# A decoder layer on one core: the softmax's divisors from a matrix product, Ln and Exp instead of VectorE's sums and reciprocal

## The chip, the cores and the metric

The kernel runs on one core of one Trainium2 chip. The metric is device time in microseconds (us) of one execution. Engines: TensorE (PE; its weight loads are shown apart as PEld), VectorE (DVE), ScalarE (ACT), GpSimd (POOL) and SyncE (SP), which only issues transfers.

## What is computed

A decoder layer over 4 sequences of 1024 rows with 256 features: a gated recurrence with one state per head (16 heads of 16), cross attention to 77 rows of context, and a feed-forward part with 2 shared and 8 routed experts, of which each row uses two. A layer norm follows each. The change touches the cross attention:

```python
q = (x @ Wq.T).reshape(B, Sq, H, Dh).transpose(0, 2, 1, 3)
k = (y @ Wk.T).reshape(B, -1, H, Dh).transpose(0, 2, 1, 3)
v = (y @ Wv.T).reshape(B, -1, H, Dh).transpose(0, 2, 1, 3)
scores = jnp.einsum('bhqd,bhkd->bhqk', q, k)
scores = jnp.where(attention_mask == 0, -1e9, scores)
attn = jax.nn.softmax(scores / sqrt(Dh), axis=-1)
out = jnp.einsum('bhqk,bhkd->bhqd', attn, v)
return out.transpose(0, 2, 1, 3).reshape(B, Sq, Dall) @ Wo.T + bo
```

The output of the recurrence enters the residual only for rows from the 683rd on; the rest of the layer does not wait for it in the earlier rows.

## The kernel before

**Tiles and periods.** The 1024 positions are taken in 8 tiles of 128; a tile holds its 128 positions of all 4 sequences ("batches" b = 0 to 3). Tiles 0 to 4 are free: they need nothing of the recurrence. Tiles 5, 6 and 7 are bound: they add the recurrence's rows after a gate, a norm and a projection (`gate_rows`, `project_rows`). The recurrence runs on VectorE over 16 superblocks of 32 step pairs; two superblocks are a period, of 128 steps (t = 0 to 127), and between superblocks VectorE lays out the next one's vectors (`lay_out`, L1558, L1565). Period p does tile p for p = 0 to 4; period 5 has no tile of its own; periods 6 and 7 do tiles 5 and 6; tile 7 comes after the recurrence, alone. Superblocks from the 10th on also form outputs (L1584), which GpSimd sums (L1194 to L1202).

**Order on VectorE.** After every step VectorE calls `attention_after(t, ...)`, which does the piece of attention, norm or routing that is due at step t by the tables `FREE_AT` (free tiles) and `BOUND_AT` (bound tiles). The queue is in order: a piece that waits for another engine holds up the recurrence. Two successive steps are one pair; the pieces of both are done after the pair.

**Order on TensorE and ScalarE.** `last_experts` runs the last five experts of the tile before, with a part ahead of each: start (preparation of a superblock), attend (queries and scores), weigh (softmax and values), finish (projection `wo`), second (another preparation, which in free tiles waits for VectorE's residual). Then come the router, the two shared experts and the first three routed experts of the own tile (in bound tiles all eight). Each pass of a routed expert is a product (L642), a Gelu (L928), a product (L651) and a copy of the result (L934). ScalarE waits in `sums` (L943) for the store of the tile before, which follows its last norm. SP loads each expert's weights when the expert two places before it is done (L296, L297); in its queue stand also the stores of the recurrence's outputs (L325).

**The softmax.** ScalarE copies the scores to `probs` (L836). The smallest of each row (scores are negated) is found by VectorE (L1359). In tiles 0 to 4 and 7 (`SHIFTED`) GpSimd subtracts it (L1107), ScalarE takes one Exp per batch (L843), and VectorE sums the weights (L1366). In tiles 5 and 6 ScalarE does 16 Exp per batch with the accumulator as the sum (L847). TensorE transposes the weights by head (L506), ScalarE copies them to `eT` (L855), and TensorE multiplies them with the values (L514) in pairs of heads, 32 rows of a bank for two heads. VectorE takes the reciprocal of the sums (L1374) and copies it 16 times per head (L1376), TensorE transposes that (L525), ScalarE copies it out of its bank (L862), and VectorE multiplies (`divided`, L1383). TensorE projects (L533, L535), and VectorE adds the residual (L1333).

## Time and profile before

| | before |
|---|---|
| median of 3 runs | 2398.67 us (2394.86 to 2398.77) |
| profiled execution, its own time | 2398.25 us |
| its span | 2396.5 us |
| mean granted clock of TensorE | 0.842 of full speed |
| busy: TensorE, VectorE, ScalarE, GpSimd | 1760.5, 2050.7, 663.5, 1192.2 us |
| chain that ended last: VectorE, TensorE, GpSimd | 61%, 17%, 8% of the span |

The span runs from the first to the last recorded instruction; the execution's own time is 1.75 us longer. Times of rows are counted from the span's start.

### The profile page before, as it was taken

To read this page: it belongs to the slowest core of one execution; us is meant where nothing else is said; L and a number is where in the kernel's file an instruction comes from. 1 tells how busy PE (TensorE), PEld (TensorE's weight loads), DVE (VectorE), ACT (ScalarE), POOL (GpSimd) and SP (SyncE) were. 2 spreads that over 40 slices of the span, in tenths; PEclk is the share of its full clock that TensorE was granted. 3 is DMA by queue.
4 is the path that set the end of the run, shared out by engine and by line. 5 is a ranking of instruction groups with operands and counts; after the bars stand their busy time and mean duration, and the time that the engine had idled before them with its cause. 6 is when DMAs were issued, how large, how long until landed. Compare 5 with 4: busy or idle time off the path is not lost.

```text
span 2396.5 us, 31981 instructions
## 1 busy us (share of the span) xinstructions
PE 1760.5 (73%) x9438; PEld 1323.5 (55%) x9438; DVE 2050.7 (86%) x5770; ACT 663.5 (28%) x1457; POOL 1192.2 (50%) x1487
## 2 busy tenths in 40 slices
PE   4248988988698879886989440258797668877983
PEld 2135766676567666765667320145585436755673
DVE  5999999999999999999999998999996989924000
ACT  2122233323332333133312110161222711224121
POOL 2544354555455545554574469473763773304203
PEclk8568998999889979999899765567899669987997
DMA  7100342334324423343234220000245003540353
GB/s 260 37 1 13 133 142 82 117 134 141 104 83 141 141 80 112 137 139 107 79 110 164 82 93 14 20 1 5 97 155 190 18 1 108 171 161 18 104 171 112
DMA packets 175111, 238.53 MB, mean 100 GB/s; under 512 B 28657, under 2 KB 148074, under 8 KB 174954
## 3 DMA queue, kind: packets, MB, share of 16 engines
q1 hardware_dynamic: 140874, 194.46, 24.3%
q10 hardware_dynamic: 27936, 25.44, 3.3%
q0 software_dynamic: 6144, 16.79, 2.2%
q8 instruction: 68, 1.11, 0.2%
q14 instruction: 89, 0.73, 0.1%
HBM read 202.09 MB, written 33.16 MB: 98 GB/s over the span
## 4 chain that ended last, share of the span: by engine, by line
DVE 61%; PE 17%; issue 8%; POOL 8%; DMA 3%; ACT 2%; SPq 0%; POOLq 0%; ACTq 0%; DVEq 0%; PEldq 0%
DVE ps L1631 13%; DVE ps L1612 12%; DVE prod L1604 9%; DVE terms L1619 8%; DVE terms L1614 5%; PE ps L651 4%; PE ps L642 3%; PE ps L587 2%; PE ps L578 2%; DVE rec_out L1558 2%; DMA pj<-in_wpT 2%; DVE rec_in L1558 2%; DVE oprod L1584 2%; DVE stats L1318 1%; PE ps L434 1%
## 5 line engine op out<-in xcount | busy, mean ns | idle before, releaser
L1631 DVE TENSOR_REDUCE ps<-terms 128x64 f32<-128x320 f32 x1024 | 448.8, 484 | 0.0
L1612 DVE TENSOR_REDUCE ps<-prod 128x16 f32<-128x272 f32 x1024 | 397.4, 433 | 0.0
L1619 DVE TENSOR_TENSOR terms<-ps,rec_out 128x256 f32<-128x256 f32 x1024 | 381.8, 415 | 0.0
L1604 DVE TENSOR_TENSOR prod<-ps,rec_in 128x256 f32<-128x256 f32 x1024 | 380.9, 414 | 0.0
L642 PE MATMUL ps<-xg,fc 128*128 128x128 f32 x2848 | 353.9, 285 | 34.0 <-PE ps L651 12.0
L642 PEld LDWEIGHTS ps<-xg,fc 128*128 128x128 f32 x2848 | 343.5, 200 | 56.1 <-issue 48.5
L651 PE MATMUL ps<-pj,hT 128*128 128x256 f32 x1424 | 344.7, 397 | 33.3 <-ACT hT L928 33.3
L651 PEld LDWEIGHTS ps<-pj,hT 128*128 128x128 f32 x1424 | 273.3, 197 | 89.3 <-ACT hT L928 52.6
L578 PE MATMUL ps<-xtf,fc 128*128 128x512 f32 x512 | 246.0, 620 | 4.7 <-ACT vec L808 3.4
L587 PE MATMUL ps<-pj,hT 128*128 128x256 f32 x1024 | 237.4, 383 | 0.0
L587 PEld LDWEIGHTS ps<-pj,hT 128*128 128x128 f32 x1024 | 195.4, 191 | 57.3 <-issue 34.4
L1614 DVE TENSOR_TENSOR terms<-ps,rec_g 128x128 f32<-128x128 f32 x512 | 194.1, 379 | 0.0
L1035 POOL TENSOR_TENSOR rstd<-mv,ln_eps 128x4 f32<-128x4 f32 x19 | 3.9, 203 | 354.6 <-DVE mv L1322 354.6
L928 ACT ACTIVATE hT<-ps 128x512 f32<-128x512 f32 x178 | 104.1, 593 | 234.1 <-PE ps L642 234.0
L506 PE MATMUL ps<-ident,probs 128*77 128x128 f32 x512 | 92.5, 348 | 97.6 <-ACT probs L843 62.9
L1318 DVE BATCH_NORM_STATS2 stats<-y_out 128x6 f32<-128x256 f32 x32 | 11.2, 412 | 178.6 <-POOL y_out L1072 178.6
L1194 POOL TENSOR_TENSOR oprod<-oprod 128x128 f32<-128x128 f32 (+1 forms) x86 | 42.1, 490 | 237.8 <-DVE oprod L1584 237.7
L578 PEld LDWEIGHTS ps<-xtf,fc 128*128 128x128 f32 x512 | 101.0, 199 | 101.6 <-issue 90.4
L879 ACT ACTIVATE hT<-ps 128x512 f32<-128x512 f32 x128 | 76.4, 597 | 291.5 <-PE ps L578 291.3
L1055 POOL DMA_INDIRECT y_back<-out_rows,rows x64 | 63.1, 987 | 173.8 <-ACTq L948 158.8
L506 PEld LDWEIGHTS ps<-ident,probs 128*77 128x77 f32 x512 | 79.1, 195 | 112.0 <-issue 88.5
L934 ACT ACTIVATE y<-ps 128x256 f32<-128x256 f32 x89 | 34.2, 384 | 330.9 <-PE ps L651 330.9
(235 smaller groups left out, 3025.9 us busy)
## 6 DMA issues: line engine op xcount, KB each, us to landing
fc<-in_wfcT SPq DMA_DIRECT2D x80, 1024.0 KB, 5.2
pj<-in_wpT SPq DMA_DIRECT2D x80, 1024.0 KB, 8.2
xg_rows<-in_rows ACTq DMA_DIRECT2D x105, 128.0 KB, 2.1
out_rows<-y ACTq DMA_DIRECT2D x89, 128.0 KB, 5.7
in_rows<-o_rows SPq DMA_DIRECT2D x2, 2176.0 KB, 17.3
out_rows<-o_rows SPq DMA_DIRECT2D x2, 2176.0 KB, 16.9
xtp<-in_xT SPq DMA_DIRECT2D x32, 128.0 KB, 2.5
xin<-in_x SPq DMA_DIRECT2D x8, 512.0 KB, 6.7
```

The lines of the kernel that those rows point to most:

```text
L506: i = nc.tensor.transpose(ps[0:SK, TURNED[nth % len(TURNED)], h * P:(h + 1) * P], probs[:, b, q * QH + h], ident[:, :])
L578: ins = mm(ps[:, UP + g % 2, :], fc[:, par, c, g * P:(g + 1) * P], x2T[:, c], start=c == 0, stop=c == KC - 1)
L587: ins = mm(ps[:, ACC + b // 2, (b % 2) * D:(b % 2 + 1) * D], hT[:, g % 4, b * P:(b + 1) * P], pj[:, par, g], start=False, stop=e == NSH - ...
L642: i = mm(ps[:, UP + g // 4, g % 4 * P:(g % 4 + 1) * P], fc[:, par, c, g * P:(g + 1) * P], xg[:, c], start=c == 0, stop=c == KC - 1)
L651: i = mm(ps[:, UP + 1, 0:D], hR[:, g], pj[:, par, g], start=g == 0, stop=g == FG - 1)
L928: fn(hT[:, k], ps[:, UP + k, :], ACT.Gelu).then_inc(gelu_done, 1)
L1558: nc.vector.transpose(dst.rearrange("p n d -> p d n"), wide).then_inc(block_laid, 1)
L1604: tt(prod[:, c % PLACED, :, cols, 0:HD], SE[:, old, cols, 0:HD].unsqueeze(1).to_broadcast([P, NV, HC, HD]), rec_in[:, c].unsqueeze(2).to_b ...
L1612: red(SE[:, old, cols, HD:EH].rearrange("p v n -> p n v"), prod[:, c % PLACED, :, cols, 0:HD + 1], AX.X, ALU.add).then_inc(step_done, 1)
L1614: tt(terms[:, :, :, NV], SE[:, old, :, 0:HD], rec_g[:, c].unsqueeze(1).to_broadcast([P, HV, HD]), ALU.mult).then_inc(decayed, 1)
L1619: tt(terms[:, cols, :, 0:NV], SE[:, old, cols, HD:EH].unsqueeze(2).to_broadcast([P, HC, HD, NV]), rec_out[:, c].unsqueeze(1).to_broadcast( ...
L1631: red(SE[:, new, cols, 0:HD], terms[:, cols, :, 0:NV + 1], AX.X, ALU.add).then_inc(step_done, 1)
```

## The change

The sums of the weights come from TensorE: beside each product of the weights with a pair of heads' values there is one with `pair_ones`, of the same shape and with ones where the values were, so that each head's sum appears on that head's 16 rows of another bank. ScalarE takes Ln of the two banks and then Exp with scale -1, which gives the divisors where `divided` reads them. VectorE's sums, the reciprocal, the widening copy, TensorE's transposes of it and ScalarE's copy go. In tiles 5 and 6 Exp no longer writes the accumulator. In free tiles the divide moves from step 55 to 59 and the last norm from 110 to 112; in bound tiles everything from the divide on moves 4 steps earlier (the gathers 3).

```diff
@@ tensors @@
+        pair_ones = sb("pair_ones", [SK, 3 * HD])
-        weight_sum = sb("weight_sum", [P, B, H])
-        rden = sb("rden", [P, B, H])
-        rden_wide = qT.rearrange("p c (b h d) -> p (c b) h d", h=H, d=HD)
@@ TensorE @@
             def weigh_values(m, b):
                 pe.wait_ge(eT_sb, m * (4 * B) + (4 * b + 4))
+                if b == 0:
+                    pe.wait_ge(acc_sb, m * 2 + 1)
                 for h in range(H):
                     rows = slice(h % 8 // 2 * 2 * HD, (h % 8 // 2 + 1) * 2 * HD)
-                    i = mm(ps[rows, WEIGHED[h // 8], b * P:(b + 1) * P], vals[:, b, h // 2, h % 2 * HD:(h % 2 + 2) * HD], eT[0:SK, h], start=h % 2 == 0, stop=h % 2 == 1,
-                           tile_position=(0, rows.start))
-                    if b == B - 1 and h % 8 == 7:
-                        i.then_inc(attT_ps, 1)
-
-            def spread_sums(m):
-
-                pe.wait_ge(widened, m + 1)
-                pe.wait_ge(acc_sb, m * 2 + 1)
-                for c in range(KC):
-                    for b in range(B):
-                        i = nc.tensor.transpose(ps[:, ACC + c, b * P:(b + 1) * P],
-                                                rden_wide[:, b, c * 8:(c + 1) * 8].rearrange("p h d -> p (h d)"), ident[:, :])
-                    i.then_inc(spread_ps, 1)
+                    for bank, pair, done in ((WEIGHED[h // 8], vals[:, b, h // 2], attT_ps), (ACC + h // 8, pair_ones, spread_ps)):
+                        i = mm(ps[rows, bank, b * P:(b + 1) * P], pair[:, h % 2 * HD:(h % 2 + 2) * HD], eT[0:SK, h], start=h % 2 == 0, stop=h % 2 == 1,
+                               tile_position=(0, rows.start))
+                        if b == B - 1 and h % 8 == 7:
+                            i.then_inc(done, 1)
@@ ScalarE @@
-                    i = fn(probs[:, b, h], probs[:, b, h], ACT.Exp, bias=least[:, b, h:h + 1], scale=-1.0,
-                           accum_out=weight_sum[:, b, h:h + 1])
+                    i = fn(probs[:, b, h], probs[:, b, h], ACT.Exp, bias=least[:, b, h:h + 1], scale=-1.0)
-            def spread_sums(m):
+            def inverse_sums(m):
                 for c in range(KC):
                     act.wait_ge(spread_ps, m * 2 + (c + 1))
-                    fn(xtf[:, c], ps[:, ACC + c, :], ACT.Copy).then_inc(spread_sb, 1)
+                    fn(xtf[:, c], ps[:, ACC + c, :], ACT.Ln).then_inc(logged, 1)
+                for c in range(KC):
+                    act.wait_ge(logged, m * 2 + (c + 1))
+                    fn(xtf[:, c], xtf[:, c], ACT.Exp, scale=-1.0).then_inc(spread_sb, 1)
@@ VectorE @@
-            def sums_of_weights(t, m, at):
-            def divisors(t, m, at):
-                sums_of_weights(t, m, at["sums"])
-                divisors(t, m, at["divisors"])
+            for i in range(3):
+                nc.vector.memset(pair_ones[:, i * HD:(i + 1) * HD], float(i != 1)).then_inc(dve_const, 1)
@@ order @@
-FREE_AT = {1: 1, "caps": 46, "minima": (40, 42, 43, 44), "sums": (48, 48, 49, 50), "divisors": 51, "divided": 55, "resid": 65, 2: 65, "routing": 83, "gather": 82, "scatter": 92, "combine": 101, 3: 110}
-BOUND_AT = {"gated": 3, 0: 3, "x_plus": 12, 1: 13, "minima": (22, 22, 23, 24), "sums": (40, 40, 41, 41), "divisors": 42, "divided": 46, "resid": 53, 2: 53, "routing": 63, "gather": 30, "scatter": 74, "combine": 41, 3: 57}
+FREE_AT = {1: 1, "caps": 46, "minima": (40, 42, 43, 44), "divided": 59, "resid": 65, 2: 65, "routing": 83, "gather": 82, "scatter": 92, "combine": 101, 3: 112}
+BOUND_AT = {"gated": 3, 0: 3, "x_plus": 12, 1: 13, "minima": (22, 22, 23, 24), "divided": 42, "resid": 49, 2: 49, "routing": 59, "gather": 27, "scatter": 70, "combine": 37, 3: 53}
```

## Rows read from the trace of the kernel before

**Rows 1.** Busy time by stage: us, engines (instructions), clock, DMA share, GB/s.

```profile
600.00:840.00 240.00, 203.81 (x1152) 155.06 (x1150) 238.64 (x682) 76.99 (x149) 127.86 (x124) 0.93 0.35 117
```

**Rows 2.** Timeline, period 1 (tile 1): start, us, engine, line, [idle before].

```profile
384.36 1.12 PE L514 MATMUL ps<-eT,vals 77*32 77x128 f32 x32 [0.79 <-ACT eT L855]
385.42 0.69 DVE L1376 COPY qT<-rden 128x1024 f32<-128x1024 f32 x1
386.17 1.09 PE L525 MATMUL ps<-ident,qT 128*128 128x128 f32 x8 [0.69 <-DVE qT L1376]
389.37 0.57 ACT L928 ACTIVATE hT<-ps 128x512 f32<-128x512 f32 x1
392.19 1.28 DVE L1383 TENSOR_TENSOR xtf<-ps,xtf 128x512 f32<-128x512 f32 x2
...
412.05 2.08 PE L535 MATMUL ps<-c_o,xtf 128*128 128x256 f32 x4
417.65 1.27 DVE L1333 TENSOR_TENSOR x<-ps,x 128x512 f32<-128x512 f32 x2
448.59 0.19 DVE L1403 TENSOR_REDUCE rone<-rt 128x4 f32<-128x32 f32 x1 [0.38 <-ACT rt L868]
```

**Rows 3.** Timeline, tiles 2 to 4; last row: list of waits (us, times, longest).

```profile
660.28 1.01 PE L428 MATMUL ps<-xtp,w_f 128*16 128x128 f32 x4 [6.99 <-DVE x L1333]
847.85 1.23 ACT L843 ACTIVATE probs<-probs 128x1232 f32<-128x1232 f32 x1 [3.13 <-POOL probs L1107]
900.24 0.61 PE L428 MATMUL ps<-xtp,w_f 128*16 128x128 f32 x4 [2.15 <-DVE x L1333]
1139.86 1.01 PE L428 MATMUL ps<-xtp,w_f 128*16 128x128 f32 x4 [7.25 <-DVE x L1333]
...
PE ps L525 <- DVE qT L1376: 8.5, 5, 3.4
```

**Rows 4.** Timeline, end of period 4: VectorE and GpSimd.

```profile
1223.58 1.41 DVE L1318 BATCH_NORM_STATS2 stats<-y_out 128x6 f32<-128x256 f32 x4 [3.68 <-POOL y_out L1072]
1245.88 1.27 POOL L1172 TENSOR_TENSOR qbuf<-qbuf,fbuf 128x512 f32<-128x512 f32 x1
1249.61 1.19 DVE L1565 STREAM_TRANSPOSE vrec<-vec 128x256 f32<-128x256 f32 x2
```

**Rows 5.** Timeline, period 7 (tile 6): VectorE and ScalarE.

```profile
1843.56 1.29 DVE L1333 TENSOR_TENSOR xin<-ps,xin 128x512 f32<-128x512 f32 x2 [18.41 <-PE ps L470]
1917.68 1.09 ACT L862 ACTIVATE xtf<-ps 128x512 f32<-128x512 f32 x2 [1.80 <-PE ps L525]
1921.07 1.27 DVE L1383 TENSOR_TENSOR xtf<-ps,xtf 128x512 f32<-128x512 f32 x2
1936.36 1.28 DVE L1333 TENSOR_TENSOR x<-ps,x 128x512 f32<-128x512 f32 x2
1947.03 2.19 DVE L1326 TENSOR_SCALAR x<-x,mv,rstd 128x256 f32<-128x256 f32 x4 [3.91 <-POOL rstd L1037]
```

**Rows 6.** Timeline after the recurrence (tile 7).

```profile
2109.94 5.36 PE L642 MATMUL ps<-xg,fc 128*128 128x128 f32 x32 [3.40 <-DMA pj<-in_wpT]
2176.90 1.12 PE L514 MATMUL ps<-eT,vals 77*32 77x128 f32 x32 [0.79 <-ACT eT L855]
2179.35 1.29 DVE L1383 TENSOR_TENSOR xtf<-ps,xtf 128x512 f32<-128x512 f32 x2 [6.23 <-ACT xtf L862]
```

**Rows 7.** VectorE's groups by line and form: busy us, mean ns.

```profile
L1366 DVE TENSOR_REDUCE weight_sum<-probs 128x16 f32<-128x1232 f32 x24 | 33.3, 1429 | 1.6 <-ACT probs L843 1.6
L1376 DVE COPY qT<-rden 128x1024 f32<-128x1024 f32 x8 | 5.8, 723 | 0.3
L1374 DVE RECIPROCAL rden<-weight_sum 128x64 f32<-128x64 f32 x8 | 4.4, 550 | 0.6
```

**Rows 8.** ScalarE's groups by line and form.

```profile
L847 ACT ACTIVATION_READ_ACCUMULATOR probs<-probs,least 128x1 f32 x128 | 24.0, 188 | 0.0
L879 ACT ACT_TABLE_LOAD x17 | 21.8, 1283 | 0.3
```

More of the change, by code:

```diff
@@ L212, in decoder_layer @@
          kv_sb, sum_seen, prep_pool, block_laid, v_placed, step_done, decayed, o_terms, o_tree, o_sums, o_ready,
-         cap_done, x1T_ps, x1T_sb, q_ps, q_sb, sc_ps, sc_sb, capped, min_done, shifted, exp_done, summed, eT_ps,
-         eT_sb, rden_done, widened, attT_ps, spread_ps, spread_sb, attT_sb, wo_ps, resid, x2T_ps, doubled, x2T_sb, rt_ps, rt_sb,
+         cap_done, x1T_ps, x1T_sb, q_ps, q_sb, sc_ps, sc_sb, capped, min_done, shifted, exp_done, eT_ps,
+         eT_sb, attT_ps, spread_ps, logged, spread_sb, attT_sb, wo_ps, resid, x2T_ps, doubled, x2T_sb, rt_ps, rt_sb,
          route, w_done, picked, pos_ps, bounds_done, bounds_seen_pe, bounds_seen_act, gx_ps, gx_sb, xo1_ps,
@@ L220, in decoder_layer @@
             pool_set pool_const dve_const ctx_k_ps ctx_v_ps ctx_done prep_a_ps prep_b_ps xf1_sb fq_sb kv_sb
-            sum_seen prep_pool block_laid v_placed step_done decayed o_terms o_tree o_sums o_ready cap_done x1T_ps x1T_sb q_ps q_sb sc_ps sc_sb capped min_done shifted exp_done summed eT_ps eT_sb rden_done widened
-            attT_ps spread_ps spread_sb attT_sb wo_ps resid x2T_ps doubled x2T_sb rt_ps rt_sb route w_done picked
+            sum_seen prep_pool block_laid v_placed step_done decayed o_terms o_tree o_sums o_ready cap_done x1T_ps x1T_sb q_ps q_sb sc_ps sc_sb capped min_done shifted exp_done eT_ps eT_sb
+            attT_ps spread_ps logged spread_sb attT_sb wo_ps resid x2T_ps doubled x2T_sb rt_ps rt_sb route w_done picked
             pos_ps bounds_done bounds_seen_pe bounds_seen_act gx_ps gx_sb xo1_ps xo1_sb gate_ps gate_sb
@@ L713, in weigh @@
                             weigh_values(m, b)
-                        spread_sums(m)
                 def finish():
@@ L983, in weigh @@
                             turn_weights(m, b)
-                        spread_sums(m)
+                        inverse_sums(m)
                 def second():
@@ L1359, in minima @@
                         red(least[:, b], probs[:, b], AX.X, ALU.min).then_inc(min_done, 1)
-            def sums_of_weights(t, m, at):
-                for b in range(B):
-                    if m in SHIFTED and t == at[b]:
-                        dve.wait_ge(exp_done, m * B + (b + 1))
-                        red(weight_sum[:, b], probs[:, b], AX.X, ALU.add).then_inc(summed, 1)
-            def divisors(t, m, at):
-                if t == at:
-                    dve.wait_ge(exp_done, m * B + B)
-                    if m in SHIFTED:
-                        dve.wait_ge(summed, SHIFTED.index(m) * B + B)
-                    nc.vector.reciprocal(rden[:, :, :], weight_sum[:, :, :]).then_inc(rden_done, 1)
-                    dve.wait_ge(rden_done, m + 1)
-                    nc.vector.tensor_copy(rden_wide[:, :, :, :], rden[:, :, :].unsqueeze(3).to_broadcast([P, B, H, HD])).then_inc(widened, 1)
             def divided(t, m, at):
@@ L1667, in _ @@
             nc.vector.memset(pass_base[:, :], 0.0).then_inc(dve_const, 1)
+            for i in range(3):
+                nc.vector.memset(pair_ones[:, i * HD:(i + 1) * HD], float(i != 1)).then_inc(dve_const, 1)
             dve.wait_ge(pool_const, 1)
             red(pair_mask[:, :], head_mask[:, :].rearrange("p (g j) -> p j g", j=QK), AX.X, ALU.add).then_inc(dve_const, 1)
-            dve.wait_ge(dve_const, 4)
+            dve.wait_ge(dve_const, 7)
             for c in range(KC):
```

## The prediction

> **What bounds the kernel now.** I read the busy time by stage first, then the waits, then for each tile the rows in order of time around the softmax. In a middle period of 240 us VectorE is busy 238.6 us [rows 1]: through tiles 0 to 4 the recurrence, with the attention work dropped between its steps, fills it. TensorE is busy 203.8 us there, but what is left is mostly its own round trips with ScalarE (product, Gelu, product) and gives nothing back. The time order shows how close the two run. In tile 1 VectorE already waits 0.38 us for the router's sigmoid, `wo` of the projection ends at 414.1 us and VectorE wants it at 417.65 [rows 2], and no wait of TensorE on VectorE lies in that tile's second half. In tiles 2, 3 and 4 TensorE waits 7.0, 2.15 and 7.25 us for VectorE's residual, and ScalarE waits up to 3.1 us for the shifted scores [rows 3]. So VectorE bounds tiles 0 to 4, with a TensorE and ScalarE chain less than 10 us per tile behind it. GpSimd is a third limit at the end of tile 4: VectorE waits 3.68 us for its combined rows, and the preparation ends at 1247.15 us, 2.46 us before the layout at 1249.61 needs it [rows 4]. In the bound tiles (5, 6) VectorE waits 18.4 us for TensorE's projection; the divide in tile 6 has 2.3 us of room behind ScalarE's copies (1918.77 to 1921.07), and the norm after it waits 3.91 us for GpSimd [rows 5]. The last 300 us have no recurrence: a serial chain that starts when VectorE's last outputs let SP load expert weights (TensorE waits 3.40 us for them), and that runs through tile 7's softmax [rows 6].
>
> **What leaves VectorE.** For each shifted tile 4 sums at 1429 ns = 5.7 us, one reciprocal of 550 ns and one widening copy of 723 ns [rows 7]: 7.0 us; started back to back, 6.9 us. Tiles 0 to 4: 34.5 us. Tiles 5 and 6 lose only reciprocal and copy, 1.3 us each. Tile 7's sums lie beside the chain and are worth nothing. Three small memsets are added at the start, under 0.3 us.
>
> **What arrives.** TensorE: 16 more products per batch. The existing 16 (32 instructions) take 1.12 us at the clock granted there [rows 2, 6], and about 1.9 us where the clock is at its lower level. They stand between two batches' transposes, in the serial loop product, transpose, ScalarE copy, so all four batches count: 4.5 to 5.3 us per tile. The 8 transposes (1.09 us) go, and with them TensorE's wait for VectorE's widening copy: 8.5 us in five tiles, 3.4 at most [rows 3]. ScalarE: two copies (1.09 us together [rows 5]) become two Ln and two Exp, 2.4 us. Gelu of this shape takes 0.57 us [rows 2], hardly another time than the copy, so I take 0.6 us for each. Ln itself is in no row; the bounds are 0.2 us (the accumulator read, the smallest row) and 1.2 us (the copy twice). It also loses 64 accumulator reads of 188 ns in each of tiles 5 and 6 [rows 8].
>
> Table loads: a load takes 1283 ns [rows 8]. Between the last Exp of a tile and its copies none is seen, before the Gelu there is one. Whether Ln and Exp share a table no row shows: between 0 and 2 extra loads per tile, 0 to 2.6 us. I take 0, as for Exp and Copy, which stand in the same stretch without a branch, and keep 1.3 to 2.6 us as a rival. The Trainium skill (ScalarE: Activation LUTs, "What ACT_TABLE_LOAD costs") speaks against the change: every switch to another set costs a 1283 ns load and about 1.4 us of drain. The load agrees with rows 8; the drain is not seen before the Gelu at 389.37. The same page ("Table sets: the hidden batching unit") lists one set with both exp and ln, under which there would be no switch at all; by the first rule without the second the sum would be some 2.7 us per switch worse.
>
> **Tile by tile, as a lead over the old times.** A step pair takes 3.04 us (copy ends 386.11, divide starts 392.19, two pairs) [rows 2]; four steps later is 6.1 us.
>
> Tile 0: TensorE has room, so the lead is 6.9 us on both engines. The divide moves by +6.1 - 6.9 = -0.8 us and the reciprocals come just about then.
>
> Tile 1: the products ended at 385.48 (384.36 + 1.12) and now end 5.3 us later at 390.8, Ln and Exp at about 392.5 (the first Ln runs under the last products), and with Gelu's table load and the warming call, 1.5 us, its first use is at 394.0, where it was 389.37 [rows 2]: the expert that follows (two passes) and all behind it slip 4.7 us. TensorE's lead falls to 2.2 us. The residual comes 13.8 us earlier on VectorE, the projection only 2.2: VectorE waits there about 8 us, less what the divide waited, and then for the sigmoid. Lead 2.2.
>
> In the other tiles the slip is smaller by what TensorE waited for the widening copy. Tile 1 had the smallest such wait, 0.7 us (386.17); the longest, 3.4 us [rows 3], takes the slip to about 1 or less. I take 2.3 and 3.4 us for tiles 2 and 3 and 0 for tile 4; the bounds are 0 and 4.7 for each.
>
> Tile 2: the softmax starts from the minima, which VectorE delivers with its lead of 2.2 (ScalarE waits 3.1 us for them in tile 3 [rows 3]), so TensorE's slips don't add up here; slip 2.3; the 7.0 us wait is used: TensorE lead 6.9, VectorE 7.6 with 0.7 us of room at the router.
>
> Tile 3: start with 7.6; slip 3.4, wait used 2.15: TensorE 6.3; VectorE 7.7, with some 1.4 us of room at the router.
>
> Tile 4: the start is now ScalarE's own, with 6.5; slip 0, wait used 7.25: 13.7 us on both [rows 3]. The cap, VectorE's own 7.7 + 6.9 = 14.6, is not reached.
>
> So of 34.5 us about 13.7 arrive. The last norm two steps later (3.0 us) takes up GpSimd's wait of 3.68, of which the layout's room of 2.46 us lets 2.5 through [rows 4]: lead 16.2.
>
> **Tiles 5 to 7.** The divide moves to step 42, two pairs of about 3.4 us earlier, with 1.3 us less work: 1921.07 - 8.1 = 1913.0. ScalarE is ready at about 1919: its reads are gone, but TensorE's double products at the lower clock take the place. VectorE waits 6 us at the divide [rows 5]. In period 6 this is mostly hidden by the 18.4 us wait at the next tile's projection; but the stores of the recurrence's outputs stand in SP's queue before the next expert load, and they wait for VectorE, so some of it is passed on. If the divide's earlier time (2 us) reached the projection, the cost would be -2.7 us; if VectorE's whole delay did, 4: I take 1.7. In period 7 that wait hides nothing. The divide at 1919 lets the residual come 2 to 3 us before 1936.36, but it stands two pairs (6.8 us) earlier in the order, so VectorE is 3.5 to 4.7 us late; GpSimd's 3.91 us can hide most [rows 5]. Cost 1.5 us (between -0.4 and 4.7). What TensorE gains there waits for its next weights, whose load stands behind VectorE's end: the 3.40 us wait grows [rows 6]. Lead 13.0.
>
> **The end.** Tile 7: four batches by 1.12 us more = 4.5 us on the chain [rows 6]. Old: transposes, copy, divide, 2.6 us from the last product (2178.02) to the divide's end (2180.64) [rows 6]; new: the first half's Ln runs under the last products, then Ln, Exp, Exp, divide, 2.5 us. Net 4.5. Lead 8.5 us.
>
> **The sum.** The profiled execution took 2398.25 us (span 2396.5), 0.4 below the median 2398.67. 2398.25 - 13.7 - 2.5 + 1.7 + 1.5 + 4.5 = 2389.75; I say 2390.
>
> **Rivals.**
> Kept (1 in 10): VectorE keeps all it sheds because experts overlap more than I think. 34.5 + 2.5 - 3.2 - 4.5 = 29.3: 2369 us. For it: VectorE's busy share [rows 1]. Against: the waits of 0.38 us and the short rooms of rows 2 and 3.
>
> Extra loads or an uncovered divide (1 in 4): two table loads in each tile put 1.3 to 2.6 us on the second chain and 1.3 on the end, or period 7's wait passes whole (5 us). 2394 to 2402 us. For it: nothing in the trace shows Ln; against: one table may hold both.
>
> TensorE's chain gives nothing back (3 in 20): the slips of 4.7, 2.3, 3.4 and 0 us add up, because weights arrive just in time or the chain is held elsewhere, and the waits of 7.0, 2.15 and 7.25 us cannot be used. The lead at tile 4 is then 6.9 - 10.4 = -3.5 instead of 13.7: 2390 + 17 = 2407 us, slower. It decides when less than 7 of these 16 us are usable; to be slower by 0.2% 14 must be lost. For it: in tile 1 TensorE has no such wait; against: in tiles 2 and 4 the wait is there in the row.
>
> The change does less than it says: no; every removed instruction is in rows 7.
>
> **Numbers.** Forecast as summed 1 in 2, its own range 2381 to 2395. A measurement tells 0.2% (4.8 us) from no change. Faster by more than that (under 2393.9): all of Kept, most of the forecast: 0.57. Within: 0.26. Slower: 0.17, the last rival and a tail of the second. Range 2375 to 2405: it leaves out most of Kept and half of the slow rival.
>
> **What would show it.** VectorE busy time down by about 43 us, but its waits up by 25 to 35: new waits at the residual of tile 1 (about 8 us), at the router's sigmoid in tiles 1 to 4, and at the divide of tiles 5 and 6 (about 6 us). TensorE's wait before the second preparation (7.0, 2.15, 7.25) gone or small. Table loads unchanged in number: if 8 or 16 more, the second rival. Tile 7's four batches 4.5 us longer. The prediction is wrong if the residual of tile 1 has no wait (then faster), or if VectorE's lead at the end of tile 4 is near zero (then slower).

## The result and the profile after

| | before | after |
|---|---|---|
| median of 4 runs each | 2397.43 us (2394.86 to 2398.77) | 2457.87 us (2450.67 to 2460.68) |
| ratio, 95% interval | | 1.024 (1.0221 to 1.0259) |
| span of the profiled execution | 2396.5 us | 2454.9 us |
| mean granted clock of TensorE | 0.842 | 0.854 |
| busy: TensorE, VectorE, ScalarE, GpSimd | 1760.5, 2050.7, 663.5, 1192.2 us | 1836.4, 2011.8, 680.9, 1188.2 us |
| chain that ended last: VectorE, TensorE, GpSimd, ScalarE | 61%, 17%, 8%, 2% | 42%, 30%, 11%, 8% |

The change makes the kernel 60 us slower; the forecast was 2390 us, and the range ended at 2405. VectorE sheds 39 us of work as expected, but TensorE has 76 us more.

The products of the softmax in tile 1, in the timeline of the changed kernel (its names at L515: `vals` for the product with values, `pair_ones` for the one with ones; the other rows are ScalarE's and VectorE's up to the residual and the router):

```profile
402.56 0.41 PE L515 MATMUL ps<-eT,vals 77*32 77x128 f32 x2 [0.68 <-ACT eT L844]
402.80 0.38 PE L515 MATMUL ps<-eT,pair_ones 77*32 77x128 f32 x2
403.02 0.41 PE L515 MATMUL ps<-eT,vals 77*32 77x128 f32 x4
403.24 0.41 PE L515 MATMUL ps<-eT,pair_ones 77*32 77x128 f32 x4
403.49 0.41 PE L515 MATMUL ps<-eT,vals 77*32 77x128 f32 x4
...
406.51 0.38 PE L515 MATMUL ps<-eT,pair_ones 77*32 77x128 f32 x2
406.82 2.01 PE L504 MATMUL ps<-ident,probs 128*77 128x128 f32 x16
...
409.58 1.28 ACT L851 ACT_TABLE_LOAD   x1
...
413.98 0.60 ACT L851 ACTIVATE xtf<-ps 128x512 f32<-128x512 f32 x1 [1.27 <-PE ps L515]
414.59 1.28 ACT L854 ACT_TABLE_LOAD   x1
415.89 1.15 ACT L854 ACTIVATE xtf<-xtf 128x512 f32<-128x512 f32 x2
416.62 1.29 DVE L1358 TENSOR_TENSOR xtf<-ps,xtf 128x512 f32<-128x512 f32 x2 [15.62 <-ACT xtf L854]
...
438.68 1.29 DVE L1325 TENSOR_TENSOR x<-ps,x 128x512 f32<-128x512 f32 x2 [2.38 <-PE ps L526]
471.11 0.18 DVE L1378 TENSOR_REDUCE rone<-rt 128x4 f32<-128x32 f32 x1 [1.84 <-ACT rt L860]
```

The 64 instructions of a batch run from 402.56 to 406.89: 4.33 us at the full clock. Before, 32 instructions took 1.12 us [rows 2, 6]. So twice the instructions take 3.9 times as long: 3.2 us more per batch, not 1.12. How, is in the rows: a product is two instructions, and on one row group (32 output rows, two heads) a product starts 0.22 to 0.25 us after the one ahead of it (402.56, 402.80, 403.02). A row with four instructions is two products side by side, the last ones of one row group and the first of the next. So two row groups overlap at most, and eight instructions take 0.47 us (403.02 to 403.49).

The weight loads (PEld) show what sets that pace:

```profile
402.56 0.14 PEld L515 LDWEIGHTS ps<-eT,vals 77*32 77x32 f32 x2 [0.92 <-ACT eT L844]
402.70 0.22 PEld L515 LDWEIGHTS ps<-eT,pair_ones 77*32 77x32 f32 x2
402.92 0.25 PEld L515 LDWEIGHTS ps<-eT,vals 77*32 77x32 f32 x4
```

Each instruction loads its weights first, 110 ns (the median; up to 178 ns at the lower clock), and behind the first product the loads of one row group stand one after the other: two loads to a product, 0.22 us. The next row group's first product starts together with the third of the run (403.02), when only the run's last product is still to be loaded.

ScalarE's Ln waits for the last product; the two table loads of 1.28 us each stand around it; and VectorE, which waited for nothing at its divide before [rows 2], stands still for 15.6 us.

The longest pieces of the chain that ended last show the same batch at the lower clock, in tiles 0, 1 and 7 (start, us, what):

```profile
132.78 7.94 PE ps L515 x64
...
390.59 7.94 PE ps L515 x64
...
2204.31 7.94 PE ps L515 x64
```

7.94 us for what would be 1.96 us of values alone: 6.0 us more. The groups by line and form count it (busy us, mean ns of one; then idle before them):

```profile
L515 PE MATMUL ps<-eT,vals 77*32 77x128 f32 x1024 | 130.8, 307 | 23.9 <-ACT eT L844 23.9
L515 PE MATMUL ps<-eT,pair_ones 77*32 77x128 f32 x1024 | 130.3, 303 | 0.0
L1358 DVE TENSOR_TENSOR xtf<-ps,xtf 128x512 f32<-128x512 f32 x16 | 10.3, 685 | 110.1 <-ACT xtf L854 110.1
L851 ACT ACT_TABLE_LOAD x8 | 10.3, 1283 | 0.1
L854 ACT ACT_TABLE_LOAD x8 | 10.3, 1283 | 0.1
L851 ACT ACTIVATE xtf<-ps 128x512 f32<-128x512 f32 x16 | 9.6, 597 | 20.2 <-PE ps L515 20.2
L854 ACT ACTIVATE xtf<-xtf 128x512 f32<-128x512 f32 x16 | 9.2, 621 | 0.1
```

The duration of one instruction (mean 307 ns against 315 ns before; the median is 273 ns in both kernels) says nothing of this: it is the distance between the batch's first start and its last that grew. Sixteen table loads are new, two in each tile, beside those of [rows 8]. The middle period in busy time, to be held against [rows 1]: VectorE falls from 238.6 to 231.2 us of 240, and is no longer full.

```profile
600.00:840.00 240.00, 208.59 (x1272) 163.35 (x1272) 231.18 (x677) 80.52 (x152) 127.88 (x125) 0.96 0.35 117
```

Where the 58 us of the span arise is read from the starts of VectorE's layouts (L1565 before, L1538 after), one at each superblock. The lead over the kernel before, in us (negative is later):

| kernel | end of period 0 | 1 | 2 | 3 | 4 | 6 | last layout | tile 7's divide |
|---|---|---|---|---|---|---|---|---|
| forecast | 6.9 | 2.2 | 7.6 | 7.7 | 16.2 | 14.5 | 13.0 | 8.5 |
| changed kernel | -9.5 | -22.5 | -22.3 | -21.6 | -20.0 | -29.8 | -38.0 | -57.5 |
| values_then_ones | 6.8 | 10.2 | 18.0 | 25.6 | 34.3 | 31.9 | 27.4 | 16.0 |
| ones_twice | 2.5 | -0.3 | 5.1 | 9.5 | 14.8 | 15.2 | 16.9 | 16.7 |
| free_only | 7.5 | 10.4 | 18.2 | 25.9 | 34.6 | 35.5 | 35.5 | 23.2 |

(Before, these layouts start at 283.46, 524.49, 764.43, 1004.11, 1249.61, 1781.53 and 1968.26, the divide at 2179.35; a lead is that minus the other kernel's. The rows below the second are experiments.) Tiles 0 and 1, where batches ran at the lower clock, lose 22.5 us; tiles 2 to 4 hold their own, VectorE's gain against TensorE's loss; tiles 5 and 6 lose 10 and 8; tile 7's softmax, on the chain with nothing beside it, loses 19.5. Each row is one profiled execution. Kernels that are the same up to tile 6 differ in lead by up to 3.9 us between two executions (before_gather_later against the kernel before: 1.9 to 3.6 us from the end of period 1 on; free_only_gather_later against free_only: 3.9 us at the end of period 1 and 3.8 us at that of period 4), so smaller differences between the leads of two rows can't be read as effects.

### The profile page after: what moved, and what is told of

Read it like the earlier page. It is cut to its first block, busy times and chain, and to the rows that moved or that the text cites. A ratio compares the mean times of both kernels' runs of the same rounds, so it can differ in the third digit from the quotient of the medians.

```text
span 2454.9 us, 33762 instructions
## 1 busy us (share of the span) xinstructions
PE 1836.4 (75%) x10398; PEld 1407.1 (57%) x10398; DVE 2011.8 (82%) x5733; ACT 680.9 (28%) x1361; POOL 1188.2 (48%) x1487
## 4 chain that ended last, share of the span: by engine, by line
DVE 42%; PE 30%; POOL 11%; ACT 8%; issue 6%; DMA 2%; SPq 1%; ACTq 0%; POOLq 0%; DVEq 0%; PEldq 0%
DVE ps L1604 9%; DVE ps L1585 8%; PE ps L515 7%; PE ps L642 7%; DVE prod L1577 6%; PE ps L633 5%; DVE terms L1592 5%; DVE terms L1587 3%; ACT eT L844 2%; PE ps L504 2%; DVE rec_out L1531 2%; DVE rec_in L1531 2%; DVE oprod L1557 1%; PE ps L569 1%; PE ps L478 1%
## 5 line engine op out<-in xcount | busy, mean ns | idle before, releaser
L578 PEld LDWEIGHTS ps<-pj,hT 128*128 128x128 f32 x1024 | 196.2, 192 | 57.5 <-issue 34.4
L1310 DVE BATCH_NORM_STATS2 stats<-y_out 128x6 f32<-128x256 f32 x32 | 11.2, 412 | 167.9 <-POOL y_out L1064 167.9
L515 PE MATMUL ps<-eT,vals 77*32 77x128 f32 x1024 | 130.8, 307 | 23.9 <-ACT eT L844 23.9
```

The lines of the kernel that those rows point to most:

```text
L515: i = mm(ps[rows, bank, b * P:(b + 1) * P], pair[:, h % 2 * HD:(h % 2 + 2) * HD], eT[0:SK, h], start=h % 2 == 0, stop=h % 2 == 1, tile_pos ...
L578: ins = mm(ps[:, ACC + b // 2, (b % 2) * D:(b % 2 + 1) * D], hT[:, g % 4, b * P:(b + 1) * P], pj[:, par, g], start=False, stop=e == NSH - ...
```

## The experiments

Each ratio is against the kernel before on the same chip; beside the experiments that one took 2399 to 2408 us. The diffs show the deciding lines alone.

| kernel | ratio (95% interval) | a batch's products at the full clock |
|---|---|---|
| the changed kernel | 1.024 (1.0221 to 1.0259) | 4.33 us |
| values_then_ones | 0.9908 (0.9889 to 0.9928) | 2.03 us |
| rotated | 0.9906 (0.9878 to 0.9934) | 1.95 us |
| old_sums_plus_ones | 1.0262 (1.0238 to 1.0287) | 4.33 us |
| old_sums_ln_exp | 1.0012 (1.0 to 1.0024) | 1.12 us |
| one_switch | 1.0214 (1.0195 to 1.0232) | 4.33 us |
| pairs_two_banks | 0.9909 (0.9891 to 0.9927) | 2.02 us |
| free_only | 0.9867 (0.9845 to 0.9888) | 2.03 us |
| bound_steps_before | 0.9907 (0.9893 to 0.9922) | 2.03 us |
| ones_twice | 0.9948 (0.9932 to 0.9964) | 2.90 us for 48 |
| norm_at_110 | 0.9871 (0.9841 to 0.99) | 2.03 us |
| free_only_gather_later | 0.9866 (0.9845 to 0.9888) | 2.03 us |
| before_gather_later | 1.0001 (0.9987 to 1.0014) | 1.12 us |

### Is it the number of products, or their order?

**values_then_ones.**

```diff
-                for h in range(H):
+                for h, sums in [(h, sums) for sums in (0, 1) for h in range(H)]:
                     rows = slice(h % 8 // 2 * 2 * HD, (h % 8 // 2 + 1) * 2 * HD)
-                    for bank, pair, done in ((WEIGHED[h // 8], vals[:, b, h // 2], attT_ps), (ACC + h // 8, pair_ones, spread_ps)):
+                    bank, pair, done = (ACC + h // 8, pair_ones, spread_ps) if sums else (WEIGHED[h // 8], vals[:, b, h // 2], attT_ps)
```

> The changed kernel with the 16 products with values of a batch issued first and then the 16 with ones, in place of turns. In the changed kernel the 32 products take 4.32 us per batch at the full clock, 7.93 at the lower one, where the 16 of before took 1.12 and 1.96. Theory 1 (taking turns puts four products in a row on the same 32 output rows, and those cannot overlap) and theory 2 (each product goes to another bank than the one ahead of it, and that breaks the overlap): both expect 2.24 us per batch at the full clock, the last tile 10 us shorter, the divide's waits shorter by 8 us or more in each tile, and 2400 to 2412 us. Theory 3 (the second 16 products are dear in any order, because of what they do to the clock or of reading the same weights): 4.3 us per batch stays, 2450 to 2460 us.

Ratio 0.9908: the same products in another order are 3.2% faster than the changed kernel (0.9908 / 1.024), and faster than the kernel before by 0.9%. The timeline of tile 4's second batch:

```profile
1070.09 1.12 PE L515 MATMUL ps<-eT,vals 77*32 77x128 f32 x32 [0.79 <-ACT eT L844]
1070.98 1.13 PE L515 MATMUL ps<-eT,pair_ones 77*32 77x128 f32 x32
```

The ones products cost 0.91 us behind the values (2.03 against 1.12), a little less than the 1.12 of the prediction. Theory 3 is out. The time is 15 us and more below what theories 1 and 2 were given: what VectorE keeps was underrated, which is taken up below.

**rotated.** The loops run over the parity of the head and then over the row groups g; each turn issues a value product on the rows of group g and a ones product on those of group g + 2 (modulo 4):

```diff
+                for c in range(KC):
+                    for odd in (0, 1):
+                        for g in range(4):
+                            for h, bank, pair, done in ((8 * c + 2 * g + odd, WEIGHED[c], vals[:, b, 4 * c + g], attT_ps),
+                                                        (8 * c + 2 * ((g + 2) % 4) + odd, ACC + c, pair_ones, spread_ps)):
```

> The changed kernel with the products of a batch in an order in which each goes to other rows than the one ahead of it (row groups 0, 2, 1, 3, 2, 0, 3, 1) and the two banks alternate at every product. Theory 1 (same rows in a row cannot overlap): at most 2.24 us per batch at the full clock, perhaps less, since no two in a row share their rows, 2395 to 2412 us. Theory 2 (alternating banks breaks the overlap): 4.3 us per batch or more, no gain, 2450 us or more. Theory 3: as theory 2.

1.95 us per batch and 0.9906; its time, too, is more than 10 us below what theory 1 was given. The start of a batch in its timeline:

```profile
1072.74 0.30 PE L518 MATMUL ps<-eT,vals 77*32 77x128 f32 x1 [0.68 <-ACT eT L847]
1072.75 0.30 PE L518 MATMUL ps<-eT,pair_ones 77*32 77x128 f32 x1
1072.75 0.30 PE L518 MATMUL ps<-eT,vals 77*32 77x128 f32 x1
1072.76 0.30 PE L518 MATMUL ps<-eT,pair_ones 77*32 77x128 f32 x1
1072.87 0.27 PE L518 MATMUL ps<-eT,vals 77*32 77x128 f32 x1
1072.88 0.27 PE L518 MATMUL ps<-eT,pair_ones 77*32 77x128 f32 x1
```

Four instructions start within 0.02 us of each other, the next four 0.13 us later, each of 0.27 to 0.30 us: the four row groups work side by side. Sixteen weight loads of 110 ns on each row group are 1.76 us of the 1.95 (an estimate from these rows): with four groups at work little more than the loads is left. The banks alternate at every product and nothing is lost, so theory 2 is out in this form. It could still be the change of bank on the same rows; two more orders separate that.

**one_switch and pairs_two_banks.** The first issues value, value, ones, ones for a pair of heads (four in a row on the same rows, one change of bank); the second issues value and ones of a head, then goes to the next rows, with the odd heads in a second round (two in a row, a change of bank in each run):

```diff
+                for h, sums in [(8 * c + 2 * g + odd, sums) for c in range(KC) for g in range(4) for sums in (0, 1) for odd in (0, 1)]:
```

> The changed kernel with the order value, value, ones, ones of a pair of heads, then the next pair: four products in a row on the same 32 rows, as in the changed kernel, but with one change of bank among them in place of three. If the run of four on the same rows is what costs: 4.3 us per batch at the full clock, as in the changed kernel, and 2450 us or more. If it is the change of bank from one product to the next on the same rows (an accumulation interrupted by the other bank's): between 2.0 and 2.8 us per batch, and under 2420 us.

> The changed kernel with value product and ones product of the same head one after the other (same rows, two banks), then the next row group; the odd heads follow when all four groups had their even ones. Runs of two on the same rows, as in the kernel before, but with a change of bank inside each run. If only runs of four cost: 2.0 us per batch. If the change of bank on the same rows costs: about 4.3 us per batch. Where the time goes follows from that: 2380 to 2390 us or 2450 us and more.

one_switch: 4.33 us per batch and 1.0214, as the changed kernel. pairs_two_banks: 2.02 us and 0.9909. Its timeline:

```profile
1080.58 0.45 PE L518 MATMUL ps<-eT,vals 77*32 77x128 f32 x8 [0.79 <-ACT eT L847]
1080.82 0.43 PE L518 MATMUL ps<-eT,pair_ones 77*32 77x128 f32 x8
1081.04 0.44 PE L518 MATMUL ps<-eT,vals 77*32 77x128 f32 x8
```

and its weight loads, eight that start within 0.08 us of each other:

```profile
1080.57 0.18 PEld L518 LDWEIGHTS ps<-eT,vals 77*32 77x32 f32 x8 [1.02 <-ACT eT L847]
```

Each row holds eight instructions, a product on each of the four row groups, and the next row starts 0.22 to 0.24 us later: the pace of one row group is that of the changed kernel, but four of them overlap in place of two. In one_switch a pair of heads has eight instructions and the next pair's first comes 0.47 us after its own (1114.47 and 1114.94):

```profile
1114.47 0.30 PE L515 MATMUL ps<-eT,vals 77*32 77x128 f32 x1
1114.57 0.27 PE L515 MATMUL ps<-eT,pair_ones 77*32 77x128 f32 x1
...
1114.94 0.30 PE L515 MATMUL ps<-eT,vals 77*32 77x128 f32 x1
```

So the run of four products on the same 32 output rows is the cause, and the change of bank is not. Runs of two, as in the kernel before, cost next to nothing (2.02 against 1.95 us without any). Runs of three were not measured.

### How much is products, how much is Ln, Exp and their tables?

**old_sums_plus_ones** is the kernel before with the ones products of the change added, in its order, and their sums unused:

```diff
+                if b == 0:
+                    pe.wait_ge(acc_sb, m * 2 + 1)
                 for h in range(H):
                     rows = slice(h % 8 // 2 * 2 * HD, (h % 8 // 2 + 1) * 2 * HD)
+                    for bank, pair in ((WEIGHED[h // 8], vals[:, b, h // 2]), (ACC + h // 8, pair_ones)):
```

> The kernel before (its sums, reciprocal, widening and steps), with the ones products issued in turns with the value products as in the changed kernel, and their result unused. It prices the products alone. If the products are the main cause of the 60 us: 32 products take 4.32 us per batch at the full clock, and the time is 2435 to 2460 us. If the main cause is the two table loads per tile and Ln and Exp, it is under 2415 us.

1.0262, 65 us (2471.35 against 2406.66; above the 2435 to 2460 that were expected), with none of the rest of the change. In tiles 0 to 6 the first batch takes 7.25 to 7.94 us and the others 4.33; in tile 7 it is the middle two that take 7.94. **old_sums_ln_exp** has Ln, Exp and their loads without the products; VectorE copies the sums without their reciprocal (0.55 us per tile less):

```diff
-                    nc.vector.reciprocal(rden[:, :, :], weight_sum[:, :, :]).then_inc(rden_done, 1)
-                    fn(xtf[:, c], ps[:, ACC + c, :], ACT.Copy).then_inc(spread_sb, 1)
+                    fn(xtf[:, c], ps[:, ACC + c, :], ACT.Ln).then_inc(rden_done, 1)
+                for c in range(KC):
+                    act.wait_ge(rden_done, m * 2 + (c + 1))
+                    fn(xtf[:, c], xtf[:, c], ACT.Exp, scale=-1.0).then_inc(spread_sb, 1)
```

> The kernel before, with VectorE copying the sums in place of their reciprocals (no reciprocal), and ScalarE taking Ln and then Exp of them where it copied. No ones products. It prices Ln, Exp and the two table loads alone: 16 loads of 1283 ns more, 2.6 + 1.3 us more per tile on ScalarE. If the products are the main cause of the 60 us: 2398 to 2410 us, most of it in the last tile (4 us) and in the bound tiles. If Ln, Exp and the loads are: 2430 us or more.

1.0012 (1.0 to 1.0024): 3 us, with the same two loads per tile:

```profile
L862 ACT ACT_TABLE_LOAD x8 | 10.3, 1283 | 0.1
L865 ACT ACT_TABLE_LOAD x8 | 10.3, 1283 | 0.1
```

The products are the whole loss; Ln, Exp and 16 loads are within 0.24% of nothing. That is their price where the divide has room: in this kernel, as before, it waits in no tile but the last.

### Where the gain of the right order goes

**free_only** uses ones products (values first), Ln and Exp in tiles 0 to 4 alone, with free steps of the change; tiles 5 to 7 and their steps are those of the kernel before.

```diff
+                for sums in (0, 1) if m < FIRST_BOUND else (0,):
```

> Ones products (values first, then ones), Ln and Exp in tiles 0 to 4 alone; tiles 5, 6 and 7 as in the kernel before, with its steps. In values_then_ones VectorE was 34.3 us ahead of the kernel before at the last layout of period 4, and 18.2 of these were given back by the end: 2.4 us in period 6, 4.5 in period 7 and 12 in tile 7's softmax. If those losses come from the change in the bound tiles, this keeps nearly all: ratio 0.984 to 0.988 (some 2362 to 2370 us beside 2397). If they come from the lead itself (weights that cannot arrive earlier, a lower clock), the ratio stays near 0.991.

0.9867, with its two variants below (0.9866, 0.9871) the best of the study: 1.3% below the kernel before, and 3.6% below the changed one (0.9867 / 1.024). VectorE's lead of 34.6 us at the end of period 4 stays at 35.5 up to the last layout; in values_then_ones 6.9 of it went in periods 6 and 7. Then the profiled execution lost 12.3 us in tile 7, whose code is that of before; this is taken up below.

**bound_steps_before** is values_then_ones with the old steps in the bound tiles:

```diff
-BOUND_AT = {"gated": 3, 0: 3, "x_plus": 12, 1: 13, "minima": (22, 22, 23, 24), "divided": 42, "resid": 49, 2: 49, "routing": 59, "gather": 27, "scatter": 70, "combine": 37, 3: 53}
+BOUND_AT = {"gated": 3, 0: 3, "x_plus": 12, 1: 13, "minima": (22, 22, 23, 24), "divided": 46, "resid": 53, 2: 53, "routing": 63, "gather": 30, "scatter": 74, "combine": 41, 3: 57}
```

> values_then_ones with the steps of the bound tiles as in the kernel before (divide 46, residual and norm 53, routing 63, and so on) in place of four earlier. It prices the move alone. My sum gave the move and the divide's wait 1.7 us in period 6 and 1.5 us in period 7: if that is right, this is 2 to 4 us faster than values_then_ones (ratio 0.989 to 0.990). If the four steps earlier are a gain of their own, it is slower by 2 us or more.

Its lead goes from 36.9 us at the end of period 4 to 38.3 at the end of period 6 and 35.8 at the last layout, where values_then_ones has 34.3, 31.9 and 27.4. In these two executions the move of four steps costs 3.8 us in period 6 and 2.0 us in period 7. The first holds in the other kernels with the move as well: rotated and pairs_two_banks lose 1.6 and 1.4 us of lead in period 6, where this one gains 1.4. The second does not: pairs_two_banks loses only 0.6 us up to the last layout. The ratio, 0.9907 where 0.989 to 0.990 was expected of a cost, shows none of it: tile 7 took 17.2 us of lead here and 11.4 there.

**ones_twice** is free_only with the 16 ones products issued twice.

```diff
-                for sums in (0, 1) if m < FIRST_BOUND else (0,):
+                for sums, last in ((0, True), (1, False), (1, True)) if m < FIRST_BOUND else ((0, True),):
-                        if b == B - 1 and h % 8 == 7:
+                        if last and b == B - 1 and h % 8 == 7:
```

> free_only with the 16 ones products of each batch issued twice in tiles 0 to 4 (the second set writes the same sums again): 0.91 us per batch more, 3.6 us per tile, 18 us of TensorE's time in all. Theory of the prediction (TensorE's chain stands right behind VectorE, so what is put on it is passed on, up to its waits): VectorE's lead at the last layout of period 4 falls from 34.6 to some 20 to 27 us, and the time rises by 8 us or more. Rival (TensorE has room, because its own stages became shorter when its waits for VectorE did, the clock staying at the full level): the lead stays above 31 us and the time within 4 us of free_only.

2.90 us per batch, 0.87 us more than free_only; 17.4 us over 20 batches, and the lead at the end of period 4 falls by 19.8 us, from 34.6 to 14.8. That is below the 20 to 27 us that were expected if it is passed on up to its waits: all is passed on, and some more from the first batches of tiles 0 and 1, which ran at the lower clock for longer. The time agrees: 0.9948 against 0.9867 is 0.8%, 19 us. The waits are VectorE's, at the divide of all five tiles, 2.6 to 5.1 us; those of tiles 1 and 3:

```profile
394.22 1.29 DVE L1396 TENSOR_TENSOR xtf<-ps,xtf 128x512 f32<-128x512 f32 x2 [5.14 <-ACT xtf L875]
870.65 1.29 DVE L1396 TENSOR_TENSOR xtf<-ps,xtf 128x512 f32<-128x512 f32 x2 [3.18 <-ACT xtf L875]
```

In free_only no such wait in tiles 0 to 4 is over 0.43 us. So with the divide at step 59 the room of TensorE's chain is about the 3.6 us per tile that the ones products take once, and whatever goes beyond it is VectorE's wait.

**norm_at_110** is free_only with the last norm of a tile back at step 110 (`3: 112` to `3: 110` in `FREE_AT`).

> free_only with the last norm of a tile in free periods at step 110, as in the kernel before, in place of 112. The prediction gave the later step 2.5 us, for a wait of VectorE for GpSimd's combined rows in period 4. If right: 2 to 3 us slower than free_only, all at the end of period 4. Rival: nothing (within 1 us in the lead at that layout), because GpSimd itself is done earlier now.

From the layout in the middle of period 4 to its end, free_only gains 2.0 us on the kernel before and norm_at_110 loses 0.6: 2.6 us for the step, against the 2.5 of the prediction. Of the other kernels with the norm at 112, five gain 1.9 to 2.3 us in that half period and bound_steps_before 3.9, so the loss stands out. The wait is back, first norm_at_110, then free_only:

```profile
1198.19 1.40 DVE L1331 BATCH_NORM_STATS2 stats<-y_out 128x6 f32<-128x256 f32 x4 [3.66 <-POOL y_out L1085]
```

```profile
1191.58 1.41 DVE L1331 BATCH_NORM_STATS2 stats<-y_out 128x6 f32<-128x256 f32 x4 [0.68 <-POOL y_out L1085]
```

The ratios (0.9871 and 0.9867) are too coarse for it. This profile's lead at the end of period 4 is 9.2 us below free_only's, and 5.6 of these are there by the end of period 1, before any such wait of VectorE for GpSimd. 4.2 of them lie in the wait at tile 1's residual, first norm_at_110, then free_only:

```profile
410.26 1.29 DVE L1346 TENSOR_TENSOR x<-ps,x 128x512 f32<-128x512 f32 x2 [6.13 <-PE ps L542]
```

```profile
405.55 1.29 DVE L1346 TENSOR_TENSOR x<-ps,x 128x512 f32<-128x512 f32 x2 [1.96 <-PE ps L542]
```

The code is the same there and TensorE's waits ahead of `wo` are the same (1.51, 0.47 and 0.61 us), but in norm_at_110 the last three groups of `wo` products took 2.07 to 2.08 us (granted clock 0.50 from 402.5 to 410) and in free_only 1.13 us (1.00).

**free_only_gather_later and before_gather_later.** In tile 7 of free_only's profile ScalarE stands still for 6.28 us, and TensorE behind it, waiting for nothing that the profile names ("remote"):

```profile
2138.17 1.22 ACT L850 ACTIVATE probs<-probs 128x1232 f32<-128x1232 f32 x1
2139.43 1.44 DVE L1379 TENSOR_REDUCE weight_sum<-probs 128x16 f32<-128x1232 f32 x1 [4.18 <-issue]
2145.68 1.56 ACT L862 ACTIVATE eT<-ps 77x512 f32<-77x512 f32 x3 [6.28 <-remote]
2146.32 1.14 PE L507 MATMUL ps<-ident,probs 128*77 128x128 f32 x4 [5.41 <-ACT eT L862]
```

VectorE's 4.18 us, which the expectation below counts in, are no such stall: its sum needs ScalarE's fourth Exp, which ends at 2139.39. GpSimd's gather of tile 6's rows runs at that time (2134.2 to 2144.3 us). The first kernel moves it in free_only, the second in the kernel before:

```diff
-            for i in range(MOVES):
-                gather(6, i)
-            for i in range(WEIGHTED):
-                combine(6, i)
             rsqrt(LN_2, 7)
             for i in range(MOVES):
                 scatter(7, i)
+            for i in range(MOVES):
+                gather(6, i)
+            for i in range(WEIGHTED):
+                combine(6, i)
```

> free_only with GpSimd's gather and combining of tile 6's rows moved behind tile 7's scatter, out of tile 7's softmax. In free_only ScalarE and VectorE stood still there for 6.3 and 4.2 us while the gather's transfers ran, waiting for nothing that the profile shows, and the clock was lower afterwards: 12 us were lost between the first value product and the divide. If the gather's transfers cause it: no such stall, 5 to 12 us faster than free_only (ratio 0.982 to 0.985). If it is something else (the place of the code): the stall stays or moves, the ratio is that of free_only, 0.987.

> The kernel before with that move of the gather alone, as the control: its profile shows no such stall in tile 7, so both theories expect no change (within 0.2%).

The stall is not in that profile, and tile 7 loses 4.0 us of lead in place of 12.3; but the ratio is the same, 0.9866 (0.9845 to 0.9888). And ones_twice and norm_at_110, which have the gather in its old place, show no such stall either (they lose 0.2 and 4.4 us). Taken over all the profiles, stalls of TensorE or ScalarE of more than 0.4 us without a named releaser (the longest is the 6.28) stand in the softmax of tile 7 in eight (values_then_ones, rotated, pairs_two_banks, one_switch, bound_steps_before, both old_sums kernels, free_only). Each begins while the gather's eight transfers are issued, while four with the gather in place (the two kernels first compared, ones_twice, norm_at_110) and the two with it moved have none. So the gather's place alone does not bring the stall, its part in it is not excluded, and moving it gains nothing that these ratios can show, where 5 to 12 us were expected. What the stall waits for stays open. It is not the only loss there: before_gather_later has no stall and loses 8.1 us in tile 7, with three of its four batches of products at 1.96 us, the lower clock, where the kernel before has 1.12 in all four.

## Why the prediction was wrong

**The step that failed** is the price of the 16 products: "The existing 16 (32 instructions) take 1.12 us", and with it "all four batches count: 4.5 to 5.3 us per tile". It took the time of a row for a property of the instruction. It is one of the order: the 16 products stand in runs of two on the same 32 rows. The diff puts the ones product between them and makes runs of four, and then all 32 products take 4.33 us (7.94 at the lower clock). The addition is 3.2 us per batch (6.0), 12.8 us per tile and more. values_then_ones shows the step as it was meant: 0.91 us per batch, less than the 1.12 named. No bound was set for this term from above, though no row showed these products in this order, and so no rival and no part of the range held it; the slower rival lost its leads elsewhere. The order was there to be read in the diff: the inner loop over `bank` leaves `rows` as it is.

**VectorE's relief** was right: 39 us less busy time against 43 named, and in the right order the lead after tile 0 is 6.8 us against 6.9. Its sign of being wrong on the slow side, a lead near zero at the end of tile 4, came true: it is -20.0 us.

**Waits.** VectorE's waits were to grow by 25 to 35 us; those at the divide alone grow by 104 (6.2 to 110.1). A wait at the divide in tiles 5 and 6 was named at about 6 us; it is 11.5 and 11.2 us there, but 15.6 to 17.1 us in tiles 0 and 1, 6.8 to 7.6 us in tiles 2 to 4, where none was expected, and 33.4 us in tile 7. values_then_ones has 5.3 us in tile 6. Of the waits named for the residual of tile 1 (8 us) and the router there is 2.4 and 1.8 us after, 1.6 and 2.0 us in values_then_ones, and 6.1 and 3.1 us in norm_at_110. TensorE's waits for the residual before the second preparation are gone after, as said, and 1.1 to 1.2 us in values_then_ones.

**Table loads.** The second rival's mechanism came true, 16 more loads of 1283 ns: the table that Ln uses here does not serve Exp. Its price is smaller than the 4 to 12 us of that rival: 3 us in all in old_sums_ln_exp, at most 5.8. Ln takes 0.60 us and Exp 0.62, as estimated. The load of 1283 ns agrees with the Trainium skill (ScalarE: Activation LUTs, "What ACT_TABLE_LOAD costs"); its drain of 1.4 us is not to be seen, since Exp starts 0.02 us after its load (414.59 + 1.28, then 415.89). The set with both functions that the same page lists under "Table sets: the hidden batching unit" was not what got loaded.

**The leads of tiles 1 and 3** would have been wrong with the right price too: the forecast let 16.2 us arrive at the end of period 4, and values_then_ones brings 34.3, near the 37.0 of the rival "Kept" (34.5 + 2.5). The seven profiled kernels in a right order, ones_twice left out, bring 4.8 to 10.8 us at the end of period 1, where 2.2 were forecast, and 25.4 to 36.9 at that of period 4. The terms that failed are the slips, 4.7 us in tile 1 and 3.4 in tile 3. They were made with the stages of TensorE as long as in the trace of before. But those had been stretched: behind many of TensorE's waits the clock stood at its lower level. In tile 3 the four groups of `wo` products (L535 before) took up to 2.08 us each; in values_then_ones:

```profile
860.15 1.13 PE L526 MATMUL ps<-c_o,xtf 128*128 128x256 f32 x4
...
865.21 1.13 PE L526 MATMUL ps<-c_o,xtf 128*128 128x256 f32 x4
...
875.51 0.61 PE L426 MATMUL ps<-xtp,w_f 128*16 128x128 f32 x4 [1.19 <-DVE x L1325]
```

Likewise the first batch of tiles 2 and 3 took 1.87 and 1.96 us for 16 products, and takes 2.02 to 2.03 for 32: at the full clock the doubling is paid by it, and the softmax of tile 3, from its first product to the end of the last, is 1.2 us longer, not 3.6. The middle period's mean clock, 0.93 in [rows 1], is 0.96:

```profile
600.00:840.00 240.00, 207.18 (x1417) 159.49 (x1415) 238.77 (x698) 85.73 (x160) 134.07 (x129) 0.96 0.35 119
```

What keeps the clock up is not shown. The shorter waits may do it, but no run changes a wait alone; norm_at_110 and free_only, compared above, have the same code and the same waits ahead of tile 1's `wo`, and the clock fell in one of them. What it costs there is shown: 4.2 us more wait at the residual, about the size of the slip of 4.7. That TensorE's chain stands close behind VectorE was right: ones_twice passes its whole addition on. The room was some 3.6 us per tile, just what the products took; the prediction had less in tiles 1 and 3.

**Tile 4 and the norm.** 8.5 us were forecast for tile 4 with the norm, 8.7 came in values_then_ones; the norm's 2.5 is 2.6. The sum's fit is in part luck: before the middle of the period VectorE gains 6.8 us, all that it sheds, where 6.0 were forecast from a lead that had been lost in tiles 1 and 3.

**Periods 6 and 7** were priced at 1.7 and 1.5 us; values_then_ones shows 2.4 and 4.5. Without the four steps period 6 costs nothing (bound_steps_before gains 1.4 there); their share of the 4.5 is not resolved. **The end:** 4.5 us were forecast, which would be 3.6 for the products at 0.91 and 1 to 2 for the loads; the changed kernel loses 19.5 there, of which 17.2 lie between the start of the first batch's products and the end of the fourth's (29.9 us against 12.7).

## What to carry to other kernels

Where small products share TensorE by output rows, the order in which they are issued is part of their price: put the products of one row group at most two in a row (four in a row is what cost here; three was not measured), and read the distance between starts, not the duration of one. Before a row's time is taken for instructions that a diff adds, ask whether they will stand in the order of that row; if not, the price is unknown and needs a bound from above. And a stage measured once may have been stretched by the lower clock: before it goes into a sum, look which level it ran at, and take the other level as the bound.

## What the runs showed of the hardware

- Products of 32 output rows each: 32 of them take 1.95 us if no two in a row share their rows, 2.02 to 2.03 with runs of two and 4.33 with runs of four, whether the runs change banks or not. Where the rows show it (the changed kernel and pairs_two_banks), a row group starts a product every 0.22 to 0.25 us at the full clock, two weight loads of 110 ns; with runs of two all four groups run side by side, with runs of four two of them. With runs of four the next row group starts together with the run's third product, with runs of two 0.01 us behind its first. So about one product can stand waiting behind the one at work on its rows while others go ahead, and more than that hold back everything behind them; this is read from the starts, and no run measured it by itself. The Trainium skill (TensorEngine Tiling (Array Packing), "Key Properties") says that tiles of the array work independently and in parallel; rotated agrees, and the runs of four show that this parallelism depends on the order.
- Ln and Exp in turn load a table each time, 1283 ns, 16 times in this kernel.
- In tile 7 profiled executions of kernels with the same code there (free_only, ones_twice, norm_at_110) lose between 0.2 and 12.3 us of lead, by stalls that no named wait explains and by the clock's level. A profile shows one execution; differences of this size in that place are not read as effects of a change.
